# Layer 0 attention: the exponent's shift as a scalar column, and both score maxima of a tile ahead of the last combination

## The reference

```python
A1 = jnp.einsum('bhqd,bhkd->bhqk', Q1, K1) * scaling
A2 = jnp.einsum('bhqd,bhkd->bhqk', Q2, K2) * scaling
attn = jax.nn.softmax(A1, axis=-1) - lam * jax.nn.softmax(A2, axis=-1)
O = jnp.einsum('bhqk,bhkd->bhqd', attn, V)
rms = jnp.sqrt(jnp.mean(O * O, axis=-1, keepdims=True) + EPS)
O = O / rms * rms_scale
```

## Time and profile before

| | us |
|---|---|
| median of 3 runs | 1874.28 |
| the profiled execution | 1878.43 |
| its span | 1876.7 |
| PE busy | 1537.9 (82%) |
| DVE busy | 1378.9 (73%) |
| ACT busy | 1064.9 (57%) |
| POOL busy | 826.1 (44%) |

### The profile page before, as it was taken

One profiled execution on the slowest core, in us unless ns is written; L12 is line 12 of the kernel. 1 busy time (PEld: TensorE's weight loads), 2 busy tenths in 40 slices (PEclk: granted clock), 3 DMA queues, 4 the chain that ended last, 5 costly groups with the idle time before them and its releaser, 6 DMA issues. The chain is left out here.

```text
span 1876.7 us, 29826 instructions
## 1 busy us (share of the span) xinstructions
PE 1537.9 (82%) x11248; PEld 1204.3 (64%) x11248; DVE 1378.9 (73%) x2770; ACT 1064.9 (57%) x2122; POOL 826.1 (44%) x720
## 2 busy tenths in 40 slices
PE   5788878888878888878998689894589758999997
PEld 4566666666666666656876477784478646666675
DVE  7888888888888888885444537767943487777782
ACT  3666666666666666664554555553344355666665
POOL 5334444444444445445403656463466562223221
PEclk9999999999999999999997899997799968999999
DMA  3545444544544444544001330003045500000000
GB/s 91 104 80 98 79 93 82 96 81 83 93 79 97 81 82 81 79 80 101 1 1 41 109 117 15 2 2 103 18 104 149 130 11 1 1 1 2 1 2 24
DMA packets 334416, 117.08 MB, mean 62 GB/s; under 512 B 281009, under 2 KB 326097, under 8 KB 334145
## 3 DMA queue, kind: packets, MB, share of 16 engines
q1 hardware_dynamic: 323664, 101.54, 26.3%
q0 software_dynamic: 8496, 12.59, 3.0%
q10 hardware_dynamic: 2112, 1.05, 0.2%
HBM read 37.53 MB, written 10.49 MB: 26 GB/s over the span
## 5 line engine op out<-in xcount | busy, mean ns | idle before, releaser
L205 PE MATMUL PS<-xh,yh 128*128 128x512 f32 x512 | 228.3, 446 | 151.1 <-ACT XNT L604 81.8
L767 POOL TENSOR_TENSOR dl<-XN,dh 128x1024 f16<-128x1024 f32 x86 | 184.2, 2142 | 293.7 <-DVE XN L739 147.3
L2117 ACT ACTIVATE ET_a<-PS 128x256 f32<-128x256 f32 (+2 forms) x512 | 220.1, 499 | 119.9 <-PE PS L2010 72.8
L604 ACT ACTIVATE G<-PS,nm 128x1024 f32<-128x1024 f32 x128 | 142.7, 1115 | 160.2 <-DVE nm L689 157.2
L604 ACT ACTIVATE XNT<-PS,nm 128x1024 f32<-128x1024 f32 x128 | 143.1, 1118 | 156.1 <-DVE nm L689 153.8
L205 PEld LDWEIGHTS PS<-xh,yh 128*128 128x128 f32 x512 | 97.4, 190 | 206.4 <-ACT XNT L604 102.3
L207 PE MATMUL PS<-xh,yl 128*128 128x512 f32 x512 | 205.8, 402 | 0.0
L206 PE MATMUL PS<-xl,yh 128*128 128x512 f32 x512 | 205.8, 402 | 0.0
L683 DVE TENSOR_REDUCE nm<-PS 128x1 f32<-128x1024 f32 x128 | 154.8, 1210 | 10.8 <-PE PS L207 10.8
L685 DVE TENSOR_REDUCE nm<-PS 128x1 f32<-128x1024 f32 x128 | 155.9, 1218 | 0.7 <-PE PS L207 0.5
L767 POOL TENSOR_TENSOR dl<-D,dh 128x1024 f16<-128x1024 f32 x42 | 89.8, 2138 | 145.0 <-DVE XN L739 145.0
(11 more groups left out here) (461 smaller groups left out, 4098.9 us busy)
## 6 DMA issues: line engine op xcount, KB each, us to landing
e_wg<-in_WgT SPq DMA_DIRECT2D x16, 256.0 KB, 2.6
e_wu<-in_WuT SPq DMA_DIRECT2D x16, 256.0 KB, 3.0
e_wd<-in_WdT SPq DMA_DIRECT2D x16, 256.0 KB, 3.9
dth<-dh SPq DMA_TRANSPOSE x128, 3.1
dtl<-dl SPq DMA_TRANSPOSE x128, 3.1
m_x_rows<-m_xs SPq DMA_DIRECT2D x1, 1472.0 KB, 4.9
m_xs<-m_x_rows SPq DMA_DIRECT2D x5, 256.0 KB, 5.1
m_y_rows<-m_xs SPq DMA_DIRECT2D x5, 256.0 KB, 3.4
```

Source lines behind the costliest of these rows:

```text
L205: e.matmul(o, l[0], r[0], start=start, stop=False)
L604: e.activation(self.E[g % 2][:, half, :], self.S[half], ACT.Exp, bias=self.nm[:, half, i:i + 1], scale=1.0, accum_out=self.ss[:, u % 3, ha ...
L767: e.tensor_tensor(self.dl[:, g % 4, :], self.D[g % 3], self.dh[:, g % 4, :], SUB).then_inc(*self.d_low.up(g))
L2117: e.activation(dst, src, ACT.Exp, scale=self.SC, bias=0.0).then_inc(*self.ex.up(it))
```

## The change

Two edits in `Attn0.dve`. Line 689 adds the head's shift with `tensor_scalar`, the shift being the scalar operand (one value for each row), where it was a `tensor_tensor` addition of two 128x1 columns. And the call `top(g, 0)` (lines 685 and 689) stands ahead of `combine(g - 1)` (line 739) in each round, where it stood behind it. Waits and signals of each instruction are the same as before.

```diff
-            e.tensor_tensor(self.nm[:, 0, i:i + 1], self.nm[:, 0, i:i + 1], self.shift[:, h:h + 1], ADD).then_inc(*self.top.up((g, 0)))
+            e.tensor_scalar(self.nm[:, 0, i:i + 1], self.nm[:, 0, i:i + 1], self.shift[:, h:h + 1], None, ADD).then_inc(*self.top.up((g, 0)))
...
                 take_out(g - self.TAIL)
+            if g < self.NG:
+                top(g, 0)
             if 0 <= g - 1 < self.NG:
                 self.combine(e, q, g - 1)
-            if g < self.NG:
-                top(g, 0)
             if g in self.jobs:
                 low(self.jobs[g])
```

## The result

| | before | after |
|---|---|---|
| median, us | 1874.86 (4 runs) | 1706.43 (4 runs, 1702.84 to 1707.93) |
| profiled execution, us | 1878.43 | 1706.67 |
| its span, us | 1876.7 | 1704.9 |
| first to last start of line 689, us | 828.0 | 657.9 |
| the same for one tile (127 steps) | 6.52 | 5.18 |

The time after is 0.9099 of the time before, 95% interval 0.9083 to 0.9116. Of the 171.8 us that the span lost, 170.1 lie between the first and the last addition; the rest of the span is 1.7 us shorter. The forecast was 1720 us and 5.30 us a tile.

What follows compares the result with a forecast made beforehand. It took a 6.40 us loop through DVE, ACT and PE as the bound. 127 steps x (6.52 - 5.30) = 155 us off 1878.43 gives 1723, less the runs' offset 1720 us; range 1690 to 1785.

Steps and rivals of the forecast that it cites:

- The addition was held by POOL's subtraction: Line 689 on DVE: held until POOL's L767 ends; moving it away saves 0.89 us a tile.
- My 0.27 us for it: Line 689: the unheld new addition takes 0.27 us, where the old one had a median of 1158 ns.
- The loop of 6.40 us: Combination, addition, ACT's exponentials, square and copy set the tile; reordered, the loop is 4.32 us, below the engines' own work.
- only the stall goes: Rival: the tile stays a chain of DVE, ACT and PE waits; 0.89 us a tile saved, 1761 us; chance 0.15.
- PE's work, 5.07 us: PE's matmuls a tile (scores, `weigh`, `meet`, `y`, weight products) sum to some 5.07 us, the tile's floor.
- DVE's work, 5.13 and with holds 5.28 us: DVE's operations a tile sum to 5.13 us; a held combination makes it 5.28, above PE's 5.07.
- The held combination, 0.15 us a tile: L739 held by POOL's L794 up to 0.7 us in one tile of eight; taken as 0.15 us a tile.
- What is late next: PE's `meet` of an even tile waits for `zl` (L693), up to 0.3 us in rounds with a split.
- L670 and L676: Rival: these small DVE operations are held instead, about 0.8 us a tile, 1819 us; chance 0.05.
- The transposes: Rival: landing grows from 3.1 to 9 us or more, tile stays 6.52 us, 1874 us; chance 0.03.
- the slower case: Rival: PE without pauses is granted less clock; at 0.70 a tile takes 7.24 us, 1965 us; chance 0.04.
- The new form held like the old (1731 us): Line 689's tensor_scalar contends with POOL too: 0.7 us in one tile of eight, 11 us over the stage.

Runs made afterwards that it cites:

- The form alone: The kernel before with the tensor_scalar addition at line 689, order untouched: 1773.0 us, ratio 0.9379.
- the kernel in which PE never waits: The changed kernel with zl (line 693) first in DVE's round and POOL's lines 791 and 794 each cut in two: 1691.70 us, ratio 0.9026.
- with less work for PE: The changed kernel without the product of low tokens and high weights in `meet` (4 of 12 matmuls): 1702.8 us, ratio 0.9020.
- Both cures of the wait: Changed kernel, separately: zl (line 693) first in DVE's round, 1698.49 us; POOL's lines 791 and 794 cut in two over four rounds, 1697.88 us.
- the order alone: The changed kernel with the old two-input addition at line 689: 1723.21 us, ratio 0.9128.
- The kernel with POOL later: The kernel before, with POOL's subtraction (line 767) also waiting for the addition that follows the combination: 1800.18 us in one run.

## Why the prediction was right, point by point

*The addition was held by POOL's subtraction.* Shown from three sides: with the subtraction later it takes 159 ns, with the other form 214 ns beside a running subtraction, and at the new place 160 ns in the old form. My 0.27 us for it was high: it lasts 0.21 us, and its step is 0.14.

*The loop of 6.40 us lets go.* Right. The form alone takes 0.94 us from the addition and 0.91 from the tile, and leaves 5.61 us a tile with DVE still waiting for ACT's square; the rival "only the stall goes", 5.63 us, is what that kernel shows. The order then brings the tile to the engines' own work.

*PE's work, 5.07 us.* Right: 5.05 in the kernel in which PE never waits.

*DVE's work, 5.13 and with holds 5.28 us.* This term was too large, and with it the forecast of 5.30, which had DVE as the engine that sets the tile. It is PE that does. For L676, L654, L693 and the addition I had added durations, where the step to the next instruction counts. In the timeline above these are 407.68 - 407.49 = 0.19 for 0.27, 408.02 - 407.68 = 0.34 for 0.42, 404.07 - 403.93 = 0.14 for 0.27; the step of L654 is 0.60 for 0.68 where no wait follows it (before the change, and with less work for PE, as from 410.90 to 411.50 there). With halves for the operations of every other tile that is 0.29 less: 4.84. The splits at lines 661 and 663, 0.53 us in every sixteenth tile, were missing from the sum and add 0.03. With 0.13 of holds DVE needs 5.00. The kernel with less work on PE bears this out: its combinations have a mean of 1.47 us, 0.19 of holds, so the sum is 4.84 + 0.03 + 0.19 = 5.06, and the tile measured 5.04. In the changed kernel the tile is then PE's 5.05 and some 0.10 for `zl`, 5.15 of the measured 5.18; the last 0.03 are open. That the forecast came within 14 us owes something to the two engines being so close: with the wrong one of them on top, the tile was off by only 0.12 us.

*The held combination, 0.15 us a tile.* It measured 0.13, but not by the pieces that I named, so that the term came out so well is in part luck. L794 holds it by about 1.0 us in each of 12 cases, more than the 0.7 I had. I had put the next combination 4.0 us behind the end of the one before, from the mean tile; in the 12 cases it comes 3.40 or 3.55 us behind, since no `y` split lies between them (L739 ends at 207.75 and the held one starts at 211.15). L791 holds it by 0.38 us in 8 of 14 cases, and POOL's power operation at line 782, which I had counted as one that may hold it, never does.

*What is late next.* `zl`, as said. The 0.3 us at most that I gave it is the 0.25 us of nine of its 20 waits. The other eleven, 0.66 to 0.89 us, carry a held combination on to PE; I had priced the holds on DVE's side alone. Both cures of the wait gain.

*The rivals.* L670 and L676 stay at 156 and 275 ns at most. The transposes land in 3.2 us where it was 3.1, and no wait of PE for them appears. The granted clock was 1.00, the 2.4 GHz level, over 550 us at 98% load, so the slower case did not come. The new form held like the old (1731 us) did not come either: 217 ns at most, with 125 additions inside POOL's subtraction in the form-only kernel. The recorded text takes as certain there what the section it names gives as possible, on conditions.

## What to carry to other kernels

A tiny instruction with a long duration and no idle time ahead of it may be held inside its engine, as line 689 was; look for an instruction of another engine that ends at the same moment. Semaphores are thus not the only place where two engines meet, as the section on the chip has it: here DVE and POOL met inside an instruction, with no semaphore between the two. When a stall lies in a loop through several engines, first put what others wait for (here the bias of the exponentials) ahead of what nobody waits for at once, and only then look at the form: the order alone gave some 168 of the 170 us, and the form alone 116. And add up an engine's work from start to start, not from durations: here the difference was 0.3 us in 5.1.

## What the runs showed of the hardware that I had not expected

The unheld addition is faster in its two-input form (159 to 160 ns) than with a scalar column (212 to 217 ns), so the new form is 0.05 us dearer, and of use only where POOL runs beside it.

Not each POOL instruction holds a two-input operation of DVE. In the changed kernel L794 (128x1024) did in 12 of 12 cases, while L782, a power of 128x8 that shows 1.67 us, did in none of 14, though it had about 1.25 us still to run. Here is one on POOL in the changed kernel:

```profile
403.65 1.67 POOL L782 TENSOR_TENSOR ff<-fb,half 128x8 f32<-128x8 f32 x1
```

The combination at 404.07 takes its usual 1.27 us beside it. The kernel with POOL later has two more cases. Its L759, a subtraction of 128x256, had 0.40 us to run when a combination started and held it by 0.21 us; its L750, a scaling of 128x128 by one value a row, had 0.38 us to run in each of 6 cases, and the combination took its usual 1.28 us. What decides, the elements, the operation or the number of inputs, was not tried. A profile's spans on POOL are rough, so it is also open how much of the 1.67 us of L782 is reading.

A held instruction ends about 0.2 us sooner than the end of POOL's record plus its own length: L739 at 211.15 ends at 213.49, POOL's L794 at 212.40, and 212.40 + 1.28 would be 213.68. The difference is 0.19 to 0.20 us in all 12 cases with L794.
